# Second attention: both heads of a query tile in one step, fp32 scores with one head on each half of the array's rows

## The reference, cut to what matters

```python
q = (ln @ Wq).reshape(b, m, h, d).transpose(0, 2, 1, 3)
kv = jnp.concatenate([xn @ Wkv, ln @ Wkv], axis=1)
kv = kv.reshape(b, n + m, 2, h, d)
k = kv[:, :, 0].transpose(0, 2, 1, 3)
v = kv[:, :, 1].transpose(0, 2, 1, 3)
qn = rmsnorm(q, qn_g) * scale
kn = rmsnorm(k, kn_g)
sim = jnp.einsum('bhid,bhjd->bhij', qn, kn)
...
attn = jax.nn.softmax(sim.astype(jnp.float32), axis=-1).astype(sim.dtype)
out = jnp.einsum('bhij,bhjd->bhid', attn, v)
out = out.transpose(0, 2, 1, 3).reshape(b, m, h * d)
return out @ Wout + bout
```

## Time and profile before

| | us |
|---|---|
| median of the runs | 2117.7 |
| profiled execution, its own time | 2118.94 |
| its span, first to last instruction | 2117.2 |
| second attention, first scores to last output projection | 617.4 to 1732.2 |
| mean granted TensorE clock of the whole | 0.941 |

### The profile page before, as it was taken

How to read it: one execution, slowest core, us unless ns; L and a number is a source line. 1 busy time by engine, 2 the same in 40 slices (tenths; PEclk the granted TensorE clock), 3 DMA queues, 4 the chain that set the end, 5 groups by cost and what they waited for, 6 DMA issues and landing times. The chain is left out here.

```text
span 2117.2 us, 40087 instructions
## 1 busy us (share of the span) xinstructions
PE 1899.5 (90%) x13656; PEld 1646.9 (78%) x13657; DVE 1326.6 (63%) x2964; ACT 1018.9 (48%) x1747; POOL 622.1 (29%) x555
## 2 busy tenths in 40 slices
PE   6788947999569999999999999999999983999994
PEld 3567947999558887887888888888788763899994
DVE  5373064767658777877787778877787874222223
ACT  3543414555245555555555555555555531444441
POOL 3200002333245432542354324432443100122220
PEclk9998958999779999999999999999999985999997
DMA  5502163111342213211321133113311218211114
GB/s 205 177 37 91 50 242 108 50 47 47 87 103 56 46 43 72 61 47 37 71 59 45 39 71 71 41 33 71 72 42 32 63 64 290 66 35 38 36 35 132
DMA packets 93711, 159.24 MB, mean 75 GB/s; under 512 B 22433, under 2 KB 54879, under 8 KB 91755
## 3 DMA queue, kind: packets, MB, share of 16 engines
q1 hardware_dynamic: 82923, 134.32, 22.6%
q0 software_dynamic: 8320, 20.65, 3.3%
q10 hardware_dynamic: 2304, 2.10, 0.3%
HBM read 71.57 MB, written 32.41 MB: 49 GB/s over the span
## 5 line engine op out<-in xcount | busy, mean ns | idle before, releaser
L1814 ACT ACTIVATE a_prob<-a_slot,a_npeak 128x848 f32<-128x848 f32 x256 | 248.5, 971 | 205.4 <-DVE a_npeak L1875 205.0
L1680 PE MATMUL a_slot<-a_KHL,a_QHL 128*128 128x424 f32 (+1 forms) x1536 | 299.1, 343 | 10.9 <-DVE a_probT L1896 9.2
L1873 DVE TENSOR_REDUCE a_part_peak<-a_slot 128x2 f32<-128x848 f32 x256 | 265.6, 1037 | 40.4 <-PE a_slot L1680 40.2
L1705 PE MATMUL a_po<-a_probT,a_V 128*64 128x256 f32 (+1 forms) x2304 | 276.8, 385 | 0.0
L1827 ACT ACTIVATE a_probT<-a_slot 128x640 f32<-128x640 f32 x256 | 180.6, 706 | 195.6 <-PE a_slot L1689 152.9
L1689 PE MATMUL a_slot<-ident,a_prob 128*128 128x128 f32 x2048 | 267.0, 274 | 0.0
L1680 PEld LDWEIGHTS a_slot<-a_KHL,a_QHL 128*128 128x128 f32 x1536 | 237.0, 190 | 36.5 <-ACT a_probT L1827 10.8
L1905 DVE CUSTOM_DVE_ANT_0 a_masked<-a_prob,a_maskr,a_latent_sum 128x253 f32<-128x253 f32 x256 | 181.2, 708 | 102.9 <-ACT a_prob L1816 88.4
L1689 PEld LDWEIGHTS a_slot<-ident,a_prob 128*128 128x128 f32 x2048 | 234.4, 142 | 8.5 <-issue 0.2
L1705 PEld LDWEIGHTS a_po<-a_probT,a_V 128*64 128x64 f32 (+1 forms) x2304 | 153.8, 136 | 83.3 <-issue 7.2
L1630 PEld LDWEIGHTS a_side<-a_W,a_latT 128*128 128x128 f32 x1536 | 193.7, 196 | 24.1 <-issue 10.8
(11 more groups left out here) (321 smaller groups left out, 3035.8 us busy)
## 6 DMA issues: line engine op xcount, KB each, us to landing
a_KHL<-a_KT SPq DMA_DIRECT2D x128, 256.0 KB, 4.4
a_QHL<-a_QT SPq DMA_DIRECT2D x128, 128.0 KB, 2.3
m_up<-_L_ffn_gate_up_proj_dram SPq DMA_DIRECT2D x8, 1024.0 KB, 9.4
m_up<-in_L_ffn_W_dram SPq DMA_DIRECT2D x8, 1024.0 KB, 9.4
m_down<-in_L_ffn_W_dram SPq DMA_DIRECT2D x8, 1024.0 KB, 12.5
a_prob_dram<-a0p_zeros SPq DMA_DIRECT2D x4, 1632.0 KB, 10.7
a_dist_dram<-a_dist SPq DMA_DIRECT2D x4, 1632.0 KB, 8.1
a_band_prob<-a_prob_dram SPq DMA_DIRECT2D x4, 1632.0 KB, 7.3
```

The costliest lines, as they stand in the source:

```text
L1680: ins = t_.matmul(out[:, i * BANK:i * BANK + hi - lo], q, KHL[:, pair.parity, h, part, lo:hi], start=part == 0, stop=part == 1)
L1705: ins = t_.matmul(po_t[h * D1:(h + 1) * D1, :], V[0:rows, pair.parity, j, h, :], probT[0:rows, gi % 2, j, h, :], start=j == PARTS[0][0], s ...
L1814: a_.activation(prob[:, u % 2, 0:2 * CUT].rearrange("p (n k) -> p n k", n=2), two_banks(slot[u % 2]), ACT.Exp, bias=bias, accum_out=latent ...
L1873: v.tensor_reduce(part[:, 0:2], two_banks(slot[u % 2]), AX.X, ALU.max).then_inc(part_peaked, 1)
```

## The change

A unit pair (u, u + 1) is now one query tile with both heads: head 0 in slot 0, head 1 in slot 1. Keys and queries stay in fp32 where the transposes put them, head 0 on partitions 0 to 63 and head 1 on 64 to 127 (`KT`, `QT`, doubled by the pair's parity). A score matmul uses one half of the array's rows; heads alternate, bank by bank. The high and low parts, their DMAs, VectorE's subtraction and GpSimd's `split` are gone. Both heads' scores are computed together, and only when both turned units of the step have been copied. The FRONT piece now stands ahead of the scores, on TensorE and on ScalarE. Two pieces, V2 and Qta, change places.

```diff
 def tile_head(u):
-    return u // 4 * 2 + u % 2, u // 2 % 2
+    return u // 2, u % 2
...
-PIECES = ["Ka", "Kb", "c", "Qa", "Qb", "V0", "Kta", "V1", "Ktb", "Qta", "Ktc", "V2", "Qtb", "V3"]
-FRONT = {0: "Ka", 2: "c", 4: "Qb", 6: "V0", 8: "V1", 10: "Qta", 12: "V2", 14: "V3"}
+PIECES = ["Ka", "Kb", "c", "Qa", "Qb", "V0", "Kta", "V1", "Ktb", "V2", "Ktc", "Qta", "Qtb", "V3"]
+FRONT = {0: "Ka", 2: "c", 4: "Qb", 6: "V0", 8: "V1", 10: "V2", 12: "Qta", 14: "V3"}
...
-        KHL = sb("KHL", [P, 2, 2, 2, W2], F32R)
-        QHL = sb("QHL", [P, 2, 2, SEQ], F32R)
+        KT, QT = sb("KT", [P, 2, KEYS]), sb("QT", [P, 2, SEQ])
...
             def body(pair):
-                spread_keys(pair, "Kta")
-                spread_keys(pair, "Ktb")
-                spread_keys(pair, "Ktc")
-                spread_queries(pair, 0)
-                spread_queries(pair, 1)
...
-                for i, lo, hi in ((2, 2 * CUT, W2), (0, 0, CUT), (1, CUT, 2 * CUT)):
-                    for part in range(2):
-                        ins = t_.matmul(out[:, i * BANK:i * BANK + hi - lo], q, KHL[:, pair.parity, h, part, lo:hi],
-                                        start=part == 0, stop=part == 1)
-                    ins.then_inc(bank_filled, 1)
+                t, _ = tile_head(u)
+                if t == 0:
+                    pe.wait_ge(act_freed, count(pair, "Qta", PIECES))
+                if t == HALF:
+                    pe.wait_ge(act_freed, count(pair, "Qtb", PIECES))
+                for i, lo, hi in ((2, 2 * CUT, KEYS), (0, 0, CUT), (1, CUT, 2 * CUT)):
+                    for h in range(2):
+                        rows = slice(h * D1, (h + 1) * D1)
+                        t_.matmul(slot[h][:, i * BANK:i * BANK + hi - lo], QT[rows, pair.parity, t * P:(t + 1) * P],
+                                  KT[rows, pair.parity, lo:hi], start=True, stop=True).then_inc(bank_filled, 1)
...
                     turn(pair, u + 1)
-                    for k in range(2):
-                        nxt = ahead(pair, u + k, 2)
-                        if nxt[0]:
-                            pe.wait_ge(probT_act, pair.g * UNITS + (u + k + 1))
-                            pe.wait_ge(probT_dve, pair.g * UNITS + (u + k + 1))
-                            score(*nxt)
                     if after and u in FRONT:
                         piece(after, FRONT[u])
+                    nxt = ahead(pair, u, 2)
+                    if nxt[0]:
+                        pe.wait_ge(probT_act, pair.g * UNITS + (u + 2))
+                        pe.wait_ge(probT_dve, pair.g * UNITS + (u + 2))
+                        score(*nxt)
...
                     first, second = ahead(pair, u, 2), ahead(pair, u, 3)
+                    if after and u in FRONT:
+                        piece(after, FRONT[u])
                     if first[0]:
                         exponentials(*first)
-                    if after and u in FRONT:
-                        piece(after, FRONT[u])
-                    if second[0]:
                         exponentials(*second)
...
+            def peaks(pair, u):
+
+                n, m = (pair.g * UNITS + u) * 3, (pair.g * UNITS + u) * 2
                 for h in range(2):
...
+                    dve.wait_ge(bank_filled, n + (h + 1))
+                    v.tensor_reduce(part_peak[:, h, 2:3], slot[h][:, 2 * BANK:2 * BANK + REST], AX.X, ALU.max).then_inc(part_peaked, 1)
+                for h in range(2):
+                    dve.wait_ge(bank_filled, n + (h + 5))
+                    v.tensor_reduce(part_peak[:, h, 0:2], two_banks(slot[h]), AX.X, ALU.max).then_inc(part_peaked, 1)
+                    dve.wait_ge(part_peaked, m + (h + 3))
+                    v.tensor_reduce(npeak[:, h:h + 1], part_peak[:, h, :], AX.X, ALU.max, negate=True).then_inc(peaked, 1)
```

More of the change, by code:

```diff
@@ L1403 @@
 LAST_TILES = range(12, 16)
-QUERY_TURNS = ["Qta", "Qtb"]
-SPLIT = ["Kta", "Ktb", "Ktc"]
-COPIED = [p for p in PIECES if p not in SPLIT]
 def count(pair, step, steps):
@@ L1733, in _ @@
             pe.wait_ge(bridge.copied, TILES)
[L1734 removed]
+            pe.wait_ge(cleared, 2)
             score(start, 0)
[L1736 removed]
             pe.wait_ge(w_out_loaded, 32)
@@ L1789, in piece @@
                     act.wait_ge(set_up, NSET)
-                if step in QUERY_TURNS:
-                    k = QUERY_TURNS.index(step)
-                    if not first:
-                        act.wait_ge(qlow, pair.g * 2 - (1 - k))
-                    a_.activation(qgam[:, k, :], side[:, :], ACT.Copy, scale=gamma[:, 0:1]).then_inc(act_freed, 1)
+                if step in ("Qta", "Qtb"):
+                    a_.activation(QT[:, pair.parity, lo * P:lo * P + BANK], side[:, :], ACT.Copy, scale=gamma[:, 0:1]).then_inc(act_freed, 1)
                 elif step in ("Ka", "Kb", "Qa", "Qb"):
@@ L1804, in piece @@
                 else:
-                    if step == "Kta" and not first:
-                        act.wait_ge(k_spread, pair.g * 192)
                     lo = {"Kta": 0, "Ktb": BANK, "Ktc": SEQ}[step]
                     hi = min(lo + BANK, KEYS)
-                    a_.activation(KT[:, 0, lo:hi], side[:, 0:hi - lo], ACT.Copy).then_inc(high, 1)
+                    a_.activation(KT[:, pair.parity, lo:hi], side[:, 0:hi - lo], ACT.Copy).then_inc(act_freed, 1)
             def exponentials(pair, u):
@@ L1969, in _ @@
             bridge.combine(dve, 14)
-            piece(start, "Kta")
             scale(start, 1)
             bridge.combine(dve, 15)
-            piece(start, "Ktb")
             for t in range(12, 16):
                 bridge.normalise(dve, t)
-            piece(start, "Ktc")
-            peak(start, 0)
-            peak(start, 1)
+            peaks(start, 0)
             def body(pair):
@@ L1983, in body @@
                     one_before, two_before = group_before(pair, u, 1), group_before(pair, u, 2)
-                    row_sum(pair, u)
                     if u % 4 == 0 and two_before[0]:
                         normalise(*two_before)
-                    row_sum(pair, u + 1)
-                    if after and u - 2 in BEHIND:
-                        piece(after, BEHIND[u - 2])
+                    row_sum(pair, u)
                     if u % 4 == 2 and one_before[0]:
@@ L1999, in body @@
                     copy_first(pair, u + 1)
-                    for k in range(2):
-                        nxt = ahead(pair, u + k, 2)
-                        if nxt[0]:
-                            peak(*nxt)
+                    nxt = ahead(pair, u, 2)
+                    if nxt[0]:
+                        peaks(*nxt)
                     if u % 4 == 2:
```

99 lines of the change are left out of this document (17 added, 82 removed).

## The result

The changed kernel took 2194.6 us, the median of four runs (2189.24 to 2197.3), against 2116.6 us for the kernel before on the same chip: ratio 1.0355, with a 95% interval from 1.0337 to 1.0372. It is slower, as forecast, but by 78 us and not by 132; the predicted range began at 2200, so the time lies outside it.

The account below looks back on a forecast made before the run. The prediction took TensorE's work and its waits to bound the second attention. 15 pairs at 7.9 us more (119), the last pair 14, less 2 at the start, gave 131 us more: 2249 us, range 2200 to 2315.

Parts of the forecast that it names:

- the score block with the way to weighing: Score matmuls of both heads, 2.20 us with the second one record behind, plus 0.28 to weighing: 2.48 us.
- the loop of waits: Scores, peaks, exponentials, turning, copies in the second attention: 9.06 us a step with a value piece.
- the pair of the kernel before: Eight steps of one pair of heads in the second attention before the change, read as 68.30 us.
- s0: Step u = 0 of a pair, set by TensorE's work: 9.90 us forecast.
- s2: Step u = 2 of a pair, set by TensorE's work: 11.06 us forecast.
- s14: Step u = 14 of a pair, bound by the wait, with keys or queries as FRONT piece: 9.96 us forecast.
- s10: Step u = 10 of a pair, bound by the wait: 9.01 us forecast.
- rival C: Score block: an fp32 record on half of the rows goes by at 0.44 ns a column; 2109 us, chance 0.08.
- The last pair: Final pair of heads, without projections: steps go from 7.03 to 9.01 us in 7 steps, 14 us more.
- The start: TensorE's wait for VectorE's key subtraction at the start goes, which gives back about 2 us.
- Rival A: Score block: row halves don't work side by side, scores take 3.70 us; 2405 us in all, chance 0.12.
- Rival B: Steps of a pair: the wait is hidden, only TensorE's added work is left; 2173 us, chance 0.08.

Follow-up runs that it names:

- a_heads_serial: Changed kernel with all three score banks of head 0 ahead of those of head 1, VectorE's peaks in that order too: 2224.1 us, ratio 1.0507.

## Why the prediction was wrong in size

The direction and the mechanism held: peak behind the joint block, TensorE idle ahead of turning, six steps set by the wait. Three sizes failed, and each made the sum too large: the score block with the way to weighing (2.48 for 2.05), the loop of waits (9.06 for 8.74) and the pair of the kernel before (68.3 for 69.1). The sum was 131; these are its terms as measured.

- *The score block*, 2.48 forecast, 2.05 measured, in every step. I had the second head run one record behind; it doesn't. The last loads start 1.24 after S0 and weighing 0.61 behind their end, at 2.05. If the gap is the 0.28 that stood there before, 1.77 is stream; the start of the peak, less the 0.40 of the earlier trace rows, gives 1.75. So no lag, and the third change of the array's division costs nothing that is seen beyond the gap known from the earlier trace rows. The lower end of the prediction's bounds (1.85, and no lag) was the nearest; the stream measures 0.1 less still. The Trainium skill, "TensorE: Matmul & The Clock Gate", Part 3, which lets tiles start some 4 ns apart, agrees with this trace; I cited it and went by the column halves instead. In the two steps set by TensorE's work this term makes nearly all of the difference: s0 9.41 for 9.90, s2 10.53 for 11.06.
- *The loop*, 9.06 forecast, 8.74 measured (and in s14, with a longer piece in it, 9.61 for 9.96). Of the 0.32, the start of the peak gives 0.12 (2.15 for 2.27: the stream is 1.75 and not 1.85) and the link between the exponentials 0.16 (1.31 for 1.47). That second link was misread: in the earlier trace rows the second exponential is late because VectorE's second peak is, with a small reduction in between; ScalarE itself is free after 1.31. The change puts that reduction ahead of both peaks, so the link shrank. a_heads_serial puts it back and has 1.47 again.
- *A pair* is then 73.2 and not 76.2: 3.0 x 15 = 45 us too many.
- *The baseline*: I measured one pair of before, 68.30, one of three without the stall of s10. The mean is 12 x 0.95 / 15 = 0.8 more, so 12 us too many. The sentence "VectorE had time" was true of the step sampled and false of s10; the splitting that the change removes was waited for in 12 pairs, and the earlier trace rows held the sign of it, which I used only for rival C.
- *The last pair*: 8.74 - 7.0 in 7 steps, 12 for 14.
- *The start*: first scores at 621.6 against 617.4, +4 where I had -2. Kernels with the changed start had their first scores from 611.9 to 621.6, those with the old start from 614.7 to 620.7, so this term can't be read from single runs; whether the start gained anything is open.

131 - 45 - 12 - 2 + 6 = 78, as measured. That it comes out so exactly is luck, since the 6 is the start term of two single traces. Read from end to end, the two traces differ by 61 us in the 15 pairs, 11 in the last, 4 at the start and 2 behind the last scores.

Rival A is dead: the halves work side by side. Rival B was wrong as a mechanism, since the wait is seen in six steps. Its 2173 lies 22 us from the measured time and the forecast's 2249 lies 54, but only because the forecast's sizes were too large. C was wrong too: an fp32 record at 0.44 ns a column would have the peak at 1.3, and it is at 2.15. The swap of V2 and Qta, which the prediction gave no price, was needed: it is worth 24 us in before's form with the FRONT piece ahead (2185.3 to 2160.9).

The range was too narrow below because the errors add up. The bound without lag gave 2223, and the misread link and the baseline, which the range had no term for, both point the same way.

## What to carry to other kernels

Where two tiles fill their banks alternately, neither is ready until both nearly are, and neither may start until both slots are free. On a loop of matmul, reduction, exponential, matmul the first costs the reduction its head start (0.46 us a step in the last pair), and the second costs the matmuls theirs (1.03). Taking work off engines that such a loop doesn't wait for gives nothing back. Before adding a link from a trace, ask which of two engines set its end, and whether the change moves that one. Take the baseline of a periodic stage over all periods, and look at a stall that occurs "12 times" in 15 periods before sampling one.

## What the runs showed of the hardware

- *Two fp32 matmuls on row halves* run side by side with no lag that is seen: from the first of 12 loads to the next block 2.05 us when the halves alternate, and 2.58 when one half's six records follow the other's.
- *VectorE held up by GpSimd.* In the trace of before, 105 of the 256 row sums (two operands in SBUF, 253 columns) had no GpSimd instruction beside them and all took 0.47 to 0.49 us. Beside a multiplication, addition or subtraction on GpSimd the order of the starts decides. 57 row sums began inside such an instruction, over 0.1 us ahead of its end, or at most 0.03 us ahead of its start; all of them ended 0.27 to 0.30 us behind its end, and 55 took over 0.6 us: one 3.41 beside the addition to `xres`, 15 up to 2.42 beside the squares (line 1571), 27 from 0.94 to 1.29 beside the additions of line 1577, and 12 from 1.41 to 1.52 beside the subtraction of line 1594. Those that began 0.07 us or more ahead took 0.48. That is why three of the 15 pairs have no stall: there the row sum began 0.11 us ahead of the subtraction ("12 of 12" in an expectation leaves them out). GpSimd is held in turn: the multiplication of line 1592 took 1.04 us with no row sum beside it, 1.16 when 0.27 us of one were left at its start, and 1.30 when 0.41 were left.
- *The power is different.* 60 row sums ran beside the power of 16 or 18 columns (3.1 us or more) and took 0.48 to 0.49. 30 of them had begun ahead of it; the other 30 began over 1.3 us behind its start and ended 0.95 us or more ahead of its end. The Trainium skill, "SBUF — State Buffer", "Who interferes with whom", says that a VectorE operation with two SBUF inputs contends with a GpSimd operation that reads SBUF, that the ports they share are an exclusive lock, and that issue order decides who blocks. The trace agrees for the tensor operations above, but the 30 inside the power show no block.
- *Copies out of PSUM* kept their mean: 686 ns in before, 691 in the changed kernel, where GpSimd has the splitting no more.
- *A wait can be a gain.* One wait added on an engine that is idle 70% of the time took 14 us off the kernel, 12 of them in the 15 pairs of the second attention.
